# Delta-rule attention and mixture of experts: the first part's three inverse roots, first transposed inverse and order of work are changed

## The reference, cut

```
x1  = layernorm(x + attention(x))        # x: 8 sequences x 512 tokens x 128
out = layernorm(x1 + moe(x1))

attention: q, k, v = silu(causal_conv4(x @ W)) ; q, k divided by their norm per head of 32
  beta = sigmoid(x @ Wb) ; Kb = k*beta ; Vb = v*beta        # chunks of 64 tokens
  A = Kb K^T ; T = inverse of (I + tril(A, -1)) ; W = T Kb ; U = T Vb
  scan over chunks: u = U - W*diag(S) ; o = q*diag(S) + (q.k) u ; S += k u^T
  o = o * rsqrt(mean(o*o) + 1e-5) * g ; attention = o @ Wo
moe: scores = sigmoid(x1 @ gate) ; groups of experts, then the 8 best of 64 experts, weights
  shared expert (2 halves of 88) + sum over 8 experts of weight * mlp_88(x1)
```

## Time and profile before

| | us |
|---|---|
| median of 3 runs | 1181.41 |
| lowest, highest | 1174.15, 1197.52 |
| span of the profiled execution | 868.7 |
| PE, DVE, ACT, POOL busy in the span | 698.5, 489.8, 322.0, 548.9 |

### The profile page before, as it was taken

The page is one execution under the profiler, slowest core; times in us unless marked ns, Lnnn a source line. Parts: engine busy times, 40 slices in busy tenths (PEclk is TensorE's granted clock), DMA queues, the critical chain, the costliest instruction groups (busy, mean ns, idle before and its releaser), DMA issues.

```text
span 868.7 us, 17014 instructions
## 1 busy us (share of the span) xinstructions
PE 698.5 (80%) x4968; PEld 606.5 (70%) x4968; DVE 489.8 (56%) x1679; ACT 322.0 (37%) x867; POOL 548.9 (63%) x558
## 2 busy tenths in 40 slices
PE   5689797979888786767799998999897888961395
PEld 3567676767676666644587898988797887960385
DVE  2437878787777777755756663444334433430275
ACT  2224233333424242313043564664545536420032
POOL 0000277777777777676777777777777777777241
PEclk9898989897979796959579998999989989895599
DMA  8202041414141413111354444444434434311695
GB/s 199 77 1 89 15 140 59 144 62 142 59 142 60 137 52 107 51 61 47 98 149 123 118 122 126 117 108 130 115 102 127 110 100 115 104 41 51 263 408 215
DMA packets 89949, 97.47 MB, mean 112 GB/s; under 512 B 21836, under 2 KB 73780, under 8 KB 89859
## 3 DMA queue, kind: packets, MB, share of 16 engines
q1 hardware_dynamic: 67043, 58.45, 23.5%
q0 software_dynamic: 20992, 36.74, 12.5%
q10 hardware_dynamic: 1824, 1.19, 0.5%
HBM read 55.02 MB, written 42.34 MB: 112 GB/s over the span
## 4 chain that ended last, share of the span: by engine, by line
PE 38%; DVE 22%; issue 15%; POOL 12%; DMA 7%; SPq 2%; ACT 2%; POOLq 0%; ACTq 0%; DVEq 0%
POOL y_dram L463 12%; DMA y_dram<-arena 4%; PE fa L1215 3%; PE fc L1140 3%; PE pb L1165 3%; PE pa L1165 2%; PE fb L1140 2%; PE ba L1145 2%; DMA arena<-y_dram 2%; DVE arena L720 2%; PE fa L1145 2%; PE bb L1140 1%; PE bb L1361 1%; PE ba L1361 1%; PE fb L1382 1%
## 5 line engine op out<-in xcount | busy, mean ns | idle before, releaser
L463 POOL DMA_INDIRECT y_dram<-arena x272 | 266.4, 979 | 83.4 <-issue 73.8
L444 POOL DMA_INDIRECT rows_dram<-rows x256 | 256.9, 1004 | 97.6 <-issue 76.4
L435 POOL TENSOR_TENSOR rstd<-var_eps,minus_half 128x2 f32<-128x2 f32 (+1 forms) x24 | 25.3, 1055 | 132.6 <-DVE var_eps L662 132.6
L618 ACT ACTIVATE arena<-weights 128x176 f32 x384 | 99.0, 337 | 13.8 <-DVE arena L1025 13.2
L1079 DVE TENSOR_TENSOR arena<-bb,arena 128x512 f32<-128x512 f32 x34 | 23.5, 691 | 75.5 <-DMA y_dram<-arena 70.9
L1140 PE MATMUL fb<-arena 128*128 128x128 f32 x384 | 53.7, 284 | 14.6 <-DVE arena L720 14.0
L1140 PEld LDWEIGHTS fb<-arena 128*128 128x128 f32 x384 | 48.8, 195 | 20.9 <-DVE arena L720 13.5
L1079 DVE TENSOR_TENSOR arena<-ba,arena 128x512 f32<-128x512 f32 x34 | 23.5, 690 | 67.1 <-DMA y_dram<-arena 63.3
L1140 PEld LDWEIGHTS fc<-arena 128*128 128x128 f32 x384 | 50.0, 197 | 15.2 <-ACT arena L522 7.7
L607 ACT ACTIVATE arena<-fb 88x512 f32<-88x512 f32 x39 | 23.1, 592 | 99.3 <-PE fc L1382 89.2
L1361 PE MATMUL bb<-weights,arena 88*128 x336 | 47.9, 293 | 14.4 <-DVE arena L1113 13.8
(11 more groups left out here) (295 smaller groups left out, 1472.6 us busy)
## 6 DMA issues: line engine op xcount, KB each, us to landing
arena<-y_dram SPq DMA_DIRECT2D x16, 1024.0 KB, 12.1
arena<-rows_dram SPq DMA_DIRECT2D x192, 76.0 KB
weights<-experts SPq DMA_DIRECT2D x16, 608.0 KB
arena<-rows_dram SPq DMA_DIRECT2D x128, 38.0 KB
y_dram<-arena POOLq DMA_INDIRECT x272
rows_dram<-rows POOLq DMA_INDIRECT x256, 2.3
xc<-x_chan SPq DMA_DIRECT2D x8, 256.0 KB, 3.9
x_res<-x_tok SPq DMA_DIRECT2D x8, 256.0 KB, 3.0
```

Of the source, the lines that this page charges most:

```text
L435: pool.tensor_tensor(rstd[b % 2][:, 0:tiles], var_eps[b % 2][:, 0:tiles], minus_half[:, 0:tiles], ALU.pow).then_inc(S.rstd_done, 1)
L444: pool.indirect_dma_start(rows_dram, bass.IndirectOffsetOnAxis(ap=slot_of(a)[:, i, k:k + 1], axis=0), rows[:, NT * a + i, :], None).then_i ...
L463: pool.indirect_dma_start(y_dram, bass.IndirectOffsetOnAxis(ap=go_to[:, t:t + 1], axis=0), y_sb[q % YRING][:, i, :], None, bounds_check=B ...
L618: ins = act.activation(w_here[n % 2][:, (parts(q) * i + h) * 2 * I:(parts(q) * i + h + 1) * 2 * I], weights[:, bass.ds(at[i], 2 * I)], ACT ...
```

## The change

The heads' norm and the root mean square get a root on ScalarE (`hrt`, `rrt`) and a reciprocal on VectorE (`hrn`, `rrn`); the layernorm of the first part gets `std` on ScalarE and `rstd`, a reciprocal, on VectorE. The constants are added inside ScalarE's instruction. `seed`, the Newton steps, L662 and L435 of the first part go. Because the Newton form gave the root with a minus sign, `norm` and `on` change their factor from -1 to 1. GpSimd has only scatters in the first part. `eyet` and VectorE's `cpt0` go; `invt0` on TensorE turns `inv` after `cp0`, and ScalarE's `cpt0` copies it. `cs` now waits for `p1` ahead of its first eight matmuls and for `p2` ahead of the other eight. All slots of `AT` and `SHARED` are new. The last part keeps the power on GpSimd, under new names.

```diff
@@ -84,27 +84,29 @@
-AT = dict(proj0a=14, proj0b=23, silu0=43, sq0=50, sum0=52, proj1a=45, proj1b=47, silu1=62, sq1=80, sum1=88, proj2a=61,
-          proj2b=65, silu2=96, sq2=104, sum2=108, proj3a=77, proj3b=100, silu3=107, sq3=109, sum3=112, seed=113,
-          newt0=114, newt1=124, newt2=125, norm=128, vb=172, kb=129, kt=133, kbt=139, eye=135, eyet=162, kt_c=141,
-          kbt_c=143, dot=178, at=145, aa=146, nat=156, cp0=153, cpt0=165, z1=160, zc1=163, inv1=170, cp1=175,
-          invt1=176, cpt1=182, z2=179, zc2=183, inv2=191, cp2=196, invt2=198, cpt2=203, z3=202, zc3=205, inv3=208,
-          cp3=216, invt3=219, cpt3=224, z4=217, zc4=223, inv4=234, cp4=236, invt4=239, cpt4=243, z5=238, zc5=247,
-          inv5=250, cp5=255, xk=263, g=264, p1=265, p2=268, cs=271, scan=272, spread=275, ts=276, y1=283, t1=285,
-          osd=287, tr=289, u=292, o=294, osq=295, rms=299, rnewt0=300, rnewt1=303, rnewt2=306, on=309, to=314,
-          to_c=318, res=296, wo=319, mom=322, rstd=326, shift=332, x1=338, x1t=339, x1t_c=344, logits=345, tanh=346,
-          sc=372, r0=358, r1=359, r2=360, r3=371, r4=373, r5=374, r6=375, r7=377, rank=380, r8=382, key0=385, key1=387,
-          key2=391)
-SPREAD = (401, 405, 406, 407, 411, 412, 422, 424, 426, 427, 438, 442, 447, 456, 457, 461, 470, 474, 475, 476, 479, 494,
-          499, 501, 502, 508, 510, 511, 521, 534, 538, 541)
+AT = dict(proj0a=10, proj0b=63.4, proj1a=72.63, proj1b=81.59, proj2a=83.6, silu0=84.07, silu1=94.35, sq0=95.07,
+          sum0=98.78, sq1=99.62, sum1=100.9, proj3a=105.5, silu2=111.06, sum2=116.18, sq2=119.17, sum3=119.5,
+          proj2b=120.76, silu3=121.18, sq3=121.18, hrn=122.53, proj3b=125.62, norm=126.04, hrt=126.13, kb=138.58,
+          kt=139.09, kt_c=144.55, kbt_c=146.84, eye=150.63, kbt=151.31, nat=156.63, at=157.06, vb=162.04, cp0=169.9,
+          aa=170.06, invt0=177.24, z1=178.93, cpt0=179.94, zc1=182.22, cp1=182.32, inv1=189.16, cpt1=192.63,
+          invt1=193.57, z2=195.63, zc2=201.53, cp2=211.22, dot=211.6, inv2=214.1, z3=220.38, invt2=222.61,
+          inv3=227.14, cp3=227.21, zc3=229.26, cpt2=229.92, invt3=235.96, z4=237.48, cpt3=240.09, zc4=240.4,
+          cp4=241.31, cpt4=242.43, inv4=243.53, cp5=249.05, zc5=252.55, invt4=255.68, z5=260.41, g=262.29, p1=265.37,
+          inv5=266.04, p2=268.46, xk=274.5, scan=280.25, cs=282.45, y1=283.63, spread=284.81, ts=290.52, tr=301.4,
+          t1=303.98, osd=310.07, u=312.79, o=313.96, rms=316.06, rrn=317.48, on=317.68, res=318.25, osq=318.69,
+          rrt=321.15, mom=327.48, to_c=328.13, to=329.49, wo=337.19, rstd=338.24, std=339.95, shift=343.89, x1=348.63,
+          x1t_c=351.11, x1t=359.18, logits=360.31, r0=360.5, r1=365.74, tanh=367.14, r2=367.52, r3=371.52, r4=375.86,
+          r5=376.43, r6=376.6, r7=376.88, sc=379.11, r8=380.99, key0=386.62, key1=387.17, key2=387.63, rank=392.19)
...
-SHARED = ({"t": 289.01, "c": 275.01, "g0": 289.02, "s0": 295.01, "m0": 309.01, "g1": 289.03, "s1": 295.02, "m1": 309.02, "d": 319.01, "a": 322.01},
-          {"t": 319.02, "c": 318.01, "g0": 319.03, "s0": 318.02, "m0": 332.01, "g1": 319.04, "s1": 338.01, "m1": 332.02, "d": 345.01, "a": 377.01},
-          {"t": 345.02, "c": 346.01, "g0": 345.03, "s0": 346.02, "m0": 391.01, "g1": 380.01, "s1": 372.01, "m1": 391.02, "d": 380.02, "a": 391.03})
+SHARED = ({"t": 241.81, "c": 243.4, "g0": 280.81, "s0": 263.29, "m0": 285.9, "g1": 285.45, "s1": 269.79, "m1": 299.31,
+           "d": 317.75, "a": 318.13},
+          {"t": 305.59, "c": 324.33, "g0": 331.52, "s0": 415.33, "m0": 372.45, "g1": 407.6, "s1": 446.15, "m1":
+           394.32, "d": 491.15, "a": 440.51},
+          {"t": 471.09, "c": 458.76, "g0": 504.62, "s0": 526.96, "m0": 565.68, "g1": 515.34, "s1": 592.82, "m1":
+           610.03, "d": 629.62, "a": 745.71})
@@ -430,9 +433,9 @@
         def _(pool):
-            def inverse_std(b, tiles=NT):
-                pool.wait_ge(S.ve_done, b + 1)
-                pool.tensor_tensor(rstd[b % 2][:, 0:tiles], var_eps[b % 2][:, 0:tiles], minus_half[:, 0:tiles],
+            def inverse_std(u):
+                pool.wait_ge(S.ve_done, u + 1)
+                pool.tensor_tensor(rstd[u % 2][:, 0:2], var_eps[u % 2][:, 0:2], minus_half[:, 0:2],
@@ -445,14 +448,13 @@
+            pool.memset(ln_eps[:, :], LN_EPS)
+            pool.memset(rms_eps[:, :], RMS_EPS)
...
-            for _, a, n in sorted([(a * CYCLE + AT["rstd"], a, -1) for a in range(B)]
-                                  + [(a * CYCLE + at, a, n) for a in range(B) for n, at in enumerate(SPREAD)]):
-                if n < 0:
-                    inverse_std(a)
-                else:
+            for a in range(B):
+                for n in range(NT * TOPK):
@@ -490,14 +492,15 @@
+                if op == "hrt":
+                    act.wait_ge(S.ss_done, NT * (a + 1))
+                    if a >= 1:
+                        act.wait_ge(S.hrn_done, a)
+                    act.activation(head_rt[:, :], head_ss[:, :], ACT.Sqrt).then_inc(S.hrt_done, 1)
...
-                if op == "eyet":
-                    if a >= 2:
-                        act.wait_ge(S.tr_mm, a - 1)
-                    act.activation(by_tile(inv_t[n]), eye, ACT.Copy).then_inc(S.eye_t_set, 1)
@@ -516,13 +519,16 @@
+                for k in range(LEVELS - 1):
+                    if op == f"cpt{k}":
+                        act.wait_ge(S.invt_mm, (LEVELS - 1) * a + k + 1)
+                        if k == 0 and a >= 2:
+                            act.wait_ge(S.tr_mm, a - 1)
+                        act.activation(inv_t[n], fa[:, :], ACT.Copy).then_inc(S.invt_done, 1)
...
                     if op == f"zc{k}":
...
-                    if op == f"cpt{k}":
-                        act.wait_ge(S.invt_mm, (LEVELS - 2) * a + k)
-                        act.activation(inv_t[n], fa[:, :], ACT.Copy).then_inc(S.invt_done, 1)
@@ -532,6 +538,17 @@
                 if op == "osq":
...
+                if op == "rrt":
+                    act.wait_ge(S.t_done, a + 1)
+                    if a >= 1:
+                        act.wait_ge(S.rrn_done, a)
+                    act.activation(rms_rt[:, :], rms_ss[:, :], ACT.Sqrt, bias=rms_eps[:, 0:1],
+                                   scale=1.0 / HD).then_inc(S.rrt_done, 1)
+                if op == "std":
+                    act.wait_ge(S.mv_done, a + 1)
+                    if a >= 2:
+                        act.wait_ge(S.rs_done, a - 1)
+                    act.activation(std[n][:, :], mean_var[n][:, :, 1], ACT.Sqrt, bias=ln_eps[:, 0:1]).then_inc(S.std_done, 1)
@@ -633,22 +650,6 @@
         def _(dve):
-            def seed(x, half, y, sem, at):
-                dve.tensor_scalar(half, x, 0.5, None, ALU.mult)
-                dve.tensor_scalar(y.bitcast(U32), x.bitcast(U32), 1, None, ALU.logical_shift_right).then_inc(sem, 1)
-                dve.wait_ge(sem, at + 1)
-                dve.tensor_scalar(y.bitcast(U32), y.bitcast(U32), -1.0, float(0x5f3759df), ALU.mult, ALU.add).then_inc(sem, 1)
-            def newton(half, y, step, sem, at):
-                dve.wait_ge(sem, at)
-                dve.tensor_tensor(step, y, y, ALU.mult).then_inc(sem, 1)
-                dve.wait_ge(sem, at + 1)
-                dve.tensor_tensor(step, step, half, ALU.mult).then_inc(sem, 1)
-                dve.wait_ge(sem, at + 2)
-                dve.scalar_tensor_tensor(out=y, in0=step, scalar=1.5, in1=y, op0=ALU.subtract, op1=ALU.mult).then_inc(sem, 1)
@@ -658,11 +659,8 @@
-                dve.wait_ge(S.mv_done, b + 1)
-                dve.tensor_scalar(var_eps[n][:, 0:tiles], mean_var[n][:, 0:tiles, 1], LN_EPS, None, ALU.add).then_inc(S.ve_done, 1)
...
             def shifted(b, tiles=NT):
-                dve.wait_ge(S.rstd_done, b + 1)
@@ -671,22 +669,21 @@
                     if op == f"sum{i}":
...
+                        if i == 0 and a >= 1:
+                            dve.wait_ge(S.hrt_done, a)
...
-                if op == "seed":
-                    dve.wait_ge(S.ss_done, NT * (a + 1))
+                if op == "hrn":
+                    dve.wait_ge(S.hrt_done, a + 1)
...
-                    seed(head_ss[:, :], half_ss[:, :], head_rn[:, :], S.rn_done, 11 * a)
-                for m in range(3):
-                    if op == f"newt{m}":
-                        newton(half_ss[:, :], head_rn[:, :], step_ss[:, :], S.rn_done, 11 * a + 2 + 3 * m)
+                    dve.reciprocal(head_rn[:, :], head_rt[:, :]).then_inc(S.hrn_done, 1)
                 if op == "norm":
-                    dve.wait_ge(S.rn_done, 11 * (a + 1))
+                    dve.wait_ge(S.hrn_done, a + 1)
...
-                    dve.scalar_tensor_tensor(out=qk, in0=qk, scalar=-1.0, in1=by_head, op0=ALU.mult,
+                    dve.scalar_tensor_tensor(out=qk, in0=qk, scalar=1.0, in1=by_head, op0=ALU.mult,
@@ -709,10 +706,6 @@
-                if op == "cpt0":
-                    dve.wait_ge(S.nat_done, a + 1)
-                    dve.wait_ge(S.eye_t_set, a + 1)
```

(34 more changed lines are left out.)

15 lines of the change are left out of this document (8 added, 7 removed).

## The result

After: 1232.24 us median (1227.64 to 1234.28) against 1182.62 for before, ratio 1.050 with a 95% interval of 1.044 to 1.056. The change makes the kernel 5% slower on this chip; the forecast was 1176 us, no change.

What follows compares the result with a forecast made beforehand. It took a TensorE-VectorE walk to bound the first part, and tied TensorE and GpSimd scatter paths, then GpSimd, the expert part. -10.0 - 1.5 - 1 + 7 = -5.5 us gave 1176 us, range 1152 to 1191.

Steps and rivals of the forecast that it cites:

- Span and what lies around it (312.7, taken as fixed): Whole kernel: forecast profiled span 863 us plus a fixed 312.7 us outside it, compared with the median, gives 1176 us.
- costs the period nothing now, as it waits between scatters; its going gives only latency: First part, GpSimd: removing its 1.06 us power does not shorten the period per sequence, only latency.
- (a to c): Three rivals: clock stays up, 1159 us (0.25); shared expert is the whole effect, 1191 (0.20); more table changes, 1200 (0.06).
- Period -1.4 us: First part, per sequence against 44.38 us: sum of stalls removed and waits added; seven times gives -10.0 us.
- the loads (+0.6): First part, ScalarE: half of one table load per sequence on the path, +0.6 us, between 0 and +2.6.
- Rival (a): First part: clock stays up, period reaches GpSimd's 40.6 us floor, 7 x -3.8 = -26.5; in all -22, 1159 us; chance 0.25.
- Table loads: ScalarE: at most two per sequence, one ahead of `hrt`, one ahead of `tanh`; ACT_TABLE_LOAD 17 times in all.
- Rival (c): ScalarE changes tables oftener: four loads, 5.1 us per sequence, two on the path, +1.4 net; 1200 us; chance 0.06.
- Head -1.5 (0 to -3): Kernel start: first sequence's Newton chain, and the layernorm's, give way to load, root and reciprocal; -1.5 us.
- From the last routing step to TensorE's first quad 26 us: Behind the routing: moved shared-expert work lengthens this stretch from 19.4 to 26 us; GpSimd idles some 7 us.
- From the first quad to the end 431 us: Expert part: the rest, from TensorE's first quad to the end, stays at 431 us.
- Total -5.5: Whole kernel: -10.0 periods, -1.5 head, -1 routing tail, +7 shared expert behind routing make -5.5 us.

Runs made afterwards that it cites:

- before_again: The kernel before, unchanged, run again for its spans; 1182.1 us, ratio 1.005.
- before_std: Against before: only the first part's layernorm root moved to ScalarE and VectorE, so GpSimd only scatters there, without wait or power; 1241.1 us, ratio 1.052.
- before_std_wait_2: Against before: layernorm root moved, GpSimd's wait for the moments kept ahead of scatter 17, no power; repeat on a chip with long executions, 1183.6 us, ratio 1.001.
- after_again: The kernel after the change, unchanged, on the chip where before takes 871 us; 843.6 us, ratio 0.968 to before.
- after_pow8: Against after: a GpSimd power on constants behind every fourth scatter, eight per train; on the chip with short executions, 908.0 us, ratio 1.042 to before.
- before_std_wait: Against before: layernorm root moved, GpSimd's wait for the moments kept ahead of scatter 17, no power; on the chip with short executions, 882.8 us, ratio 1.013.
- after_pow8_2: Against after: eight GpSimd powers on constants per train, one behind every fourth scatter; repeat on a chip with long executions, 1062.1 us, ratio 0.895 to before.

## Why the prediction was wrong

The first step that failed stands in the paragraph "Sum": "Span and what lies around it (312.7, taken as fixed)". The page said 868.7 us and the times 1181, and I took the difference for something outside of the span. It is inside: before_again has a span of 1177.5 and the same work. A quarter of the time that was to be explained was in no row that I read, and every term was priced from rows of another kind of execution.

The second step that failed, and the one that gave the time its direction, is a sentence on GpSimd: the power on GpSimd (1.06 us) "costs the period nothing now, as it waits between scatters; its going gives only latency". On B the wait ahead of that power is what lets the others work: the period was forecast to fall by 1.4 us and rose from 63.4 to 71.1. Wait and power taken out cost 59 us (before_std), and the wait alone gives them back (before_std_wait_2). No rival had this: all three (a to c) priced TensorE's clock, its waits and ScalarE's loads.

On chip A, which the prediction described without knowing it, point by point from after_again:

- Period -1.4 us: measured 45.2 to 41.5, -3.7. The stall before `xk` is gone as forecast, before `cs` 1.80 (2.0 forecast), before `ts` 0.25, before `logits` 0.69 (0.85), before `rank` none. Mis-sized were the loads (+0.6), behind which no wait of TensorE stands, and above all the clock, which is left out of the sum. It still falls to the lower level after the stall before `cs`, but for a shorter time:

```profile
184.00:186.00 2.00, 2.00 (x11) 2.00 (x11) 0.76 (x5) 0.00 (x0) 1.70 (x2) 0.50 0.21 75
...
190.00:192.00 2.00, 2.00 (x17) 1.78 (x16) 1.00 (x2) 0.00 (x0) 1.69 (x2) 1.00 0.12 41
```

  The trace's clock records have it at 0.5 for 10.2 us in a sequence of before and for 3.4 or 6.8 us in one of after_again. By an estimate at half the pace that is 1.7 to 3.4 us per sequence, of the 2.3 by which the sum was short.
- Rival (a), with a chance of a quarter, has the right size: 7 x -3.7 = -26 (its price -26.5). Its mechanism holds only in part, and the rest is luck: the clock does not stay up, it falls for less long, and GpSimd's 40.6 us are no floor of the period, as after_pow8 shows.
- Table loads: 8 ahead of `hrt`, 8 ahead of `tanh` and 7 ahead of `silu`, three changes per sequence, not two, and 25 loads in all with two of the shared expert, not 17. The groups of ScalarE in after_again:

```profile
L499 ACT ACT_TABLE_LOAD x8 | 10.3, 1283 | 0.1
L572 ACT ACT_TABLE_LOAD x8 | 10.3, 1283 | 0.2
L487 ACT ACT_TABLE_LOAD x7 | 9.0, 1283 | 0.1
```

  Rival (c) feared them at +1.4 per sequence; no wait of TensorE is put down to one here, though in the old slots the layernorm's root with two loads per sequence went along with 1.5 us (before_std_wait). The Trainium skill ("ScalarE: Activation LUTs", "Table sets: the hidden batching unit") sets the root apart from the others, and the trace agrees that it needs a load; that `tanh` and `silu` then need one each the trace of before, with one load, had not shown. The order decides: in before_std_wait, where a `silu` is the first behind the root, `tanh` needs no load. The drain of 1380 ns in rival (c) does not show: a load runs from 180.78 to 182.06 us, with ScalarE's instructions before and behind it up to 180.77 and from 182.08.
- Head -1.5 (0 to -3): measured 101.3 to 95.5, -5.8.
- From the last routing step to TensorE's first quad 26 us: measured 410.9 - 386.4 = 24.5 (19.4 before). GpSimd idles there for 3 us, forecast 7.
- From the first quad to the end 431 us: measured 842.5 - 410.9 = 431.6.
- Total -5.5: measured 843.6 - 871.1 = -27.5; rival (a)'s -22 and the 4.3 of the head give -26.3.

So most terms of the walk were good to some microseconds on A, with the clock left out of the sum and the likeliest case chosen wrong, and the walk did not apply to the chip on which the time was taken.

What is shown: on B the scatters of GpSimd starve the other engines; the wait in the middle of a train, and much more so a compute instruction behind each fourth scatter, relieves them in the first part; the change took the wait and the one power of before away. What is only argued: how a scatter holds an instruction up on another engine. It is not the DMA's bandwidth (62 GB/s while all stands still, 107 on A). A hint, no more: traces of B hold some 8,000 records of semaphore updates, those of A 19,000, for the same work, and nearly all that is missing are landings of DMAs (5,768 in after, 16,689 in after_again). That is also a reason why the waits on B have no releaser. The number goes with the chip and not with the starving: after_pow8_2 holds 8,646. The Trainium skill says in "NOTIFIC — the notification-queue block", "7.1 Overflow: three behaviours, one of which stalls the engine", that a full queue of such records can be set to stop the engine that writes them. No run here shows that it does so here, nor whether an execution that records nothing would be starved.

## What to carry to other kernels

Before anything is argued from a profile, hold its span against the times: here the two were 1.8 us apart in every run with both on record, and the gap of 312.7 us meant that the trace was of another kind of execution than the one to be predicted. The first run to ask for is then the kernel itself once more. An instruction that looks idle on an engine off the path (a wait, a power of 1 us) may be what paces that engine's DMAs; before it is taken out, look at what the other engines do during its unbroken trains. Where GpSimd issues indirect DMAs in long trains (32 here), try a cheap compute instruction every fourth one: against before, here it costs 4% on one chip and gives 10% on another, and only a run on each tells.

Two rates that agree need not be cause and effect. On A the trains took 41.4 us and the sequences 41.5; only the kernel with longer trains showed that neither bound the other.
